# An attention and expert block on one core: a rebuilt head, half of the first attention group in step 0, and one exponential over four score banks in place of two

## The chip, the cores and the metric

The kernel runs on one core of one Trainium2 chip. Its engines work at the same time from queues of their own: TensorE (PE, with its weight loads PEld), VectorE (DVE), ScalarE (ACT), GpSimd (POOL), and SyncE (SP), which here only issues DMAs. They wait for each other on semaphores. The metric is device time in microseconds (us); lower is better. The profile is of one execution; its span runs from the first to the last instruction.

## The reference

For 16 batches of 256 tokens with 128 channels, one block of an adaptive-norm transformer in fp32:

```python
mod = (silu(c) @ wmod).reshape(16, 6, 1, 128)          # shifts, scales and gates
h = layernorm(x) * (1 + ca) + sa
q, k, v = split(h @ Wqkv + bqkv)                       # 16 heads of 8
Kmat = exp(-(|k|^2 + |q|^2 - 2 k.q) * r_sigma)         # 256 x 256 for each head, no softmax
x = x + ga * ((Kmat @ v) @ Wproj + bproj)
h = layernorm(x) * (1 + cb) + sb
mask = top2(softmax(h @ Wr.T + br))                    # 2 of 8 experts
x = x + gb * sum_e mask_e * (h @ We_e.T + be_e)
```

The gates ga and gb are pushed away from zero to at least 0.25 in size.

## The kernel before

One batch is one unit of work. The 16 heads of a batch are handled in four groups of four; a group's scores are 256 x 256 for four heads and fill four banks of PSUM (`scores`, 128 partitions x 4 banks x 512). Per group, TensorE computes the scores (`qk_scores`, line 962: eight matmuls, two token halves by four heads, each with 32 rows of `st`), ScalarE takes the exponential from PSUM into `probs` (`exp`, line 495, two instructions of 128 x 1024, one for two banks each), and TensorE multiplies with the values (`pv`, line 982, eight matmuls, four for each token half). The squares |q|^2 and |k|^2 are brought into the scores by extra rows of `st`: `st` has, for a head, the query or key in a high and a low fp32r part, and rows with the norms and with ones. These rows are gathered by DMAs (`stack` in the sync block, lines 310 to 322).

The order is written out by hand, in steps: step k does the attention of batch k, and beside it the query and key rows of batch k+1 (`qk_rows`, line 1001, and then bias, high and low parts, squares and norms), the layernorm of batch k+2, the projection and second norm of batch k-1, and router and experts of batches k-2 and k-3. Each engine has its own list for a step, with semaphore waits where it needs the others. Steps 0 to 2 lack the later parts and have less TensorE work. Ahead of step 0 is the head (steps -2 and -1): modulation, layernorm of batch 0, queries and keys of batch 0, their norms, and the DMAs that fill `st` for batch 0. At its end stands the last step (`last`) and a `tail`.

In the head, a few things matter here:

- `warm_up` (line 914) issues matmuls of the identity matrix whose results nobody reads. They stand in the head, and in step 0 three behind `qk_scores(0, 1)` and two behind `norms(1)`.
- Queries and keys of batch 0 go into one bank `qkv_ps`; VectorE adds the bias for both (`qkf`, line 714), squares both (639), and makes the low parts (641); ScalarE makes the high parts (475); TensorE makes the norms from the squares into `qkv_ps` (1023); VectorE copies their high part (726) and makes the low one (731). Then the norm rows go to `st` by a DMA from SP (317) and one from ScalarE's queue (488).
- The bias columns for queries and keys (`bias_columns`, lines 646 to 659) need `bq_all` from memory and stand behind the modulation columns (`modulation`, lines 626 and 627), which `h1` of batch 0 (553) waits for.
- VectorE clears `vpad` of batch 0 (903).
- `qk_scores` of a group waits in two places: for the exponential of the group before over banks 0 and 1 (`exp_a`) ahead of its first matmul, and over banks 2 and 3 (`exp_b`) ahead of its third:

## Time and profile before

| | us |
|---|---|
| runs | 222.79, 222.18, 224.8 |
| median | 222.79 |
| profiled execution, its device time | 223.4 |
| profiled execution, its span | 221.6 |
| PE busy in the span | 211.3 (95%) |
| DVE busy | 176.4 (80%) |
| ACT busy | 163.5 (74%) |
| POOL busy | 138.3 (62%) |

The device time of the profiled execution is 1.8 us more than its span, and 0.6 us more than the median. On the chain of work that ended last, PE has 88% of the span, ACT 3%, DVE, POOL and plain issue 2% each, DMA 1%. A matmul's shown duration is longer than the distance to the next one, since matmuls are pipelined: for how fast TensorE goes, the distance of starts counts. The view of the granted clock is in tenths of full speed; half of it is the lower of the two levels, 1.2 GHz, and all of it 2.4 GHz.

### The profile page before, as it was taken

Reading aid. Unit: us, or ns where it says so; the run is one execution under the profiler, and the core shown is the slowest. Engines: PE = TensorE matmul, PEld = TensorE weight load, DVE = VectorE, ACT = ScalarE, POOL = GpSimd, SP = SyncE. Lnnn points to the kernel's source line nnn. Section 1 sums busy time; section 2 is a strip of 40 time slices with the busy share of each in tenths; the row PEclk is TensorE's granted clock in tenths of the full one; section 3 lists DMA queues with packets and bytes.
Section 4 is the critical chain, followed back from the end, with each engine's and each line's share of the span. In section 5 each row is a group of like instructions: output and inputs, shape, how many; then the busy total and the mean of one; then the engine's idle time right before and its main releaser. Section 6 shows DMA issues by size and latency. Waiting matters only on the chain.

```text
span 221.6 us, 8225 instructions
## 1 busy us (share of the span) xinstructions
PE 211.3 (95%) x3250; PEld 148.2 (67%) x3250; DVE 176.4 (80%) x610; ACT 163.5 (74%) x234; POOL 138.3 (62%) x204
## 2 busy tenths in 40 slices
PE   7979889899999999999999999999999999999993
PEld 6656454567676767677677767676767767666791
DVE  5876442768888898988898888889898889877884
ACT  5236888877877868698877788686879777787362
POOL 5455756564957758575849486675857594434183
PEclk9996999999999999999999999999999999999999
DMA  5565233332323332434333332324341423200001
GB/s 152 150 209 180 71 114 104 114 105 104 114 74 127 106 119 86 151 89 148 96 144 74 104 129 81 125 81 143 86 151 68 149 67 120 79 24 27 3 24 49
DMA packets 22472, 22.94 MB, mean 104 GB/s; under 512 B 2330, under 2 KB 20258, under 8 KB 22434
## 3 DMA queue, kind: packets, MB, share of 16 engines
q1 hardware_dynamic: 21962, 21.79, 30.3%
q10 hardware_dynamic: 472, 0.62, 0.9%
q8 instruction: 26, 0.43, 0.8%
q14 instruction: 12, 0.10, 0.2%
HBM read 6.65 MB, written 2.12 MB: 40 GB/s over the span
## 4 chain that ended last, share of the span: by engine, by line
PE 88%; ACT 3%; issue 2%; DVE 2%; POOL 2%; DMA 1%; POOLq 0%; DVEq 0%; ACTq 0%
PE att_ps L982 26%; PE scores L962 12%; PE qkv_ps L1001 7%; PE qkv_ps L1010 4%; PE qkv_ps L1120 3%; PE mid_ps L1048 3%; PE ffn_ps L1120 3%; PE ffn_ps L1122 3%; PE ffn_ps L1121 3%; ACT probs L495 3%; PE att_ps L1120 2%; PE scores L914 2%; PE mid_ps L1084 2%; PE qkv_ps L1122 2%; PE qkv_ps L1121 2%
## 5 line engine op out<-in xcount | busy, mean ns | idle before, releaser
L495 ACT ACTIVATE probs<-scores 128x1024 f32<-128x1024 f32 x128 | 124.3, 1022 | 12.1 <-PE scores L962 7.1
L982 PE MATMUL att_ps<-probs,vpad 128*32 128x256 f32 x1024 | 68.0, 382 | 0.0
L982 PEld LDWEIGHTS att_ps<-probs,vpad 128*32 128x32 f32 x1024 | 29.6, 109 | 17.7 <-issue 0.2
L962 PE MATMUL scores<-st 32*128 32x256 f32 x512 | 37.3, 329 | 4.2 <-ACT probs L495 2.7
L368 POOL TENSOR_TENSOR ve<-stats,eps 128x2 f32<-128x2 f32 x32 | 6.3, 195 | 44.8 <-DVE stats L688 44.8
L708 DVE SCALAR_TENSOR_TENSOR acc<-ffn_ps,mask,acc 128x128 f32<-128x128 f32 x114 | 32.0, 343 | 0.2
L962 PEld LDWEIGHTS scores<-st 32*128 32x128 f32 x512 | 23.1, 183 | 13.2 <-ACT probs L495 4.7
L411 POOL TENSOR_TENSOR sq<-qkf 128x512 f32<-128x512 f32 x15 | 15.6, 1042 | 20.8 <-DVE qkf L714 20.8
L375 POOL TENSOR_SCALAR xn<-x_all,stats,rstd 128x128 f32<-128x128 f32 x30 | 25.8, 863 | 1.6
L370 POOL TENSOR_TENSOR rstd<-ve,expo 128x2 f32<-128x2 f32 x32 | 22.8, 711 | 2.5
L708 DVE SCALAR_TENSOR_TENSOR acc<-qkv_ps,mask,acc 128x128 f32<-128x128 f32 x64 | 18.0, 344 | 7.3 <-PE qkv_ps L1122 7.3
L714 DVE TENSOR_TENSOR qkf<-qkv_ps,bqk_col 128x512 f32<-128x512 f32 x16 | 11.1, 692 | 12.1 <-PE qkv_ps L1001 12.0
L413 POOL TENSOR_TENSOR hl<-qkf,hl 128x512 fp32r<-128x512 f32 x15 | 19.4, 1292 | 0.0
L1001 PE MATMUL qkv_ps<-h,wqk_sb 128*32 128x256 f32 x256 | 17.1, 385 | 0.0
L1120 PE MATMUL ffn_ps<-we_hi,h_hi 128*128 128x256 f32 x56 | 17.1, 305 | 0.0
L502 ACT COPY acc<-mid_ps 128x256 f32<-128x256 f32 x15 | 5.6, 372 | 14.8 <-PE mid_ps L1084 14.8
L1121 PE MATMUL ffn_ps<-we_hi,h_lo 128*128 128x256 f32 x56 | 15.6, 279 | 0.0
L1122 PE MATMUL ffn_ps<-we_lo,h_hi 128*128 128x256 f32 x56 | 15.6, 279 | 0.0
L708 DVE SCALAR_TENSOR_TENSOR acc<-att_ps,mask,acc 128x128 f32<-128x128 f32 x52 | 14.6, 343 | 0.2 <-DVE acc L708 0.2
L382 POOL TENSOR_TENSOR gated<-acc,rb_all 128x256 f32<-128x256 f32 x14 | 10.3, 737 | 5.2 <-DVE acc L708 4.5
L688 DVE BATCH_NORM_STATS2 stats<-x_all 128x6 f32<-128x256 f32 x32 | 12.5, 423 | 0.1
L396 POOL TENSOR_TENSOR x_all<-x_all,rb_all 128x256 f32<-128x256 f32 x16 | 11.8, 739 | 0.0
(172 smaller groups left out, 429.6 us busy)
## 6 DMA issues: line engine op xcount, KB each, us to landing
st<-hl SPq DMA_DIRECT2D x47, 256.0 KB
rb_all<-rb_rows SPq DMA_DIRECT2D x16, 192.0 KB, 3.2
out_dram<-x_all SPq DMA_DIRECT2D x16, 128.0 KB, 1.8
x_all<-in_L_attn_x_dram SPq DMA_DIRECT2D x13, 128.0 KB, 3.0
st<-norm_parts SPq DMA_DIRECT2D x60, 16.0 KB
we_sb<-in_L_ffn_w_experts_dram SPq DMA_DIRECT2D x1, 512.0 KB, 5.4
w_mod_sb<-in_L_wmod_dram SPq DMA_DIRECT2D x1, 256.0 KB, 4.6
st<-hl ACTq DMA_DIRECT2D x1, 256.0 KB
```

The costliest lines, as they stand in the source:

```text
L370: nc.gpsimd.tensor_tensor(rstd[:, n, :], ve[:, n, :], expo[:, :], ALU.pow).then_inc(rstd_ok, 1)
L375: i = nc.gpsimd.tensor_scalar(xn[:, par, t * C:(t + 1) * C], x_all[:, b, t * C:(t + 1) * C], stats[:, 0, par, 3 * t + 1:3 * t + 2], rstd[: ...
L411: nc.gpsimd.tensor_tensor(sq[:, :, :], qkf[:, :, :], qkf[:, :, :], ALU.mult).then_inc(sq_ok, 1)
L413: nc.gpsimd.tensor_tensor(hl[:, 1:4:2, :], qkf[:, :, :], hl_f[:, 0:4:2, :], ALU.subtract).then_inc(lo_ok, 1)
L495: nc.scalar.activation(probs[:, g, 2 * half:2 * half + 2, :], scores[:, 2 * half:2 * half + 2, :], ACT.Exp, scale=two_sigma).then_inc((exp ...
L708: v.scalar_tensor_tensor(acc[:, q, t, :], y, m, acc[:, q, t, :], ALU.mult, ALU.add).then_inc(acc_step, 1)
L962: i = pe.matmul(scores[:, r, t * T:(t + 1) * T], st[rows, par, g, t * P:(t + 1) * P], st[rows, par, g, T:2 * T], start=True, stop=True)
L982: i = pe.matmul(att_ps[r * ROWS:(r + 1) * ROWS, 0:T], heads[:, g * ROWS:(g + 1) * ROWS], probs[:, g, r, t * T:(t + 1) * T], start=(g == 0 ...
L1001: i = pe.matmul(qkv_ps[m, a * T:(a + 1) * T], wqk_sb[:, a, m], h1[:, :], start=True, stop=True)
L1120: pe.matmul(dst, hi, we_hi[:, es], start=True, stop=False)
L1121: pe.matmul(dst, lo, we_hi[:, es], start=False, stop=False)
L1122: i = pe.matmul(dst, hi, we_lo[:, es], start=False, stop=True)
```

## The change

Three things are changed.

1. The exponential is one instruction of 128 x 2048 over all four banks of a group. It waits for both halves of the scores (`qk_a`, `qk_b`) and signals once (`exp_done`). `qk_scores` waits once, for all of it, and its wait ahead of the third matmul is gone.
2. In step 0 the five warm-up matmuls are gone, and the first token half of `pv(0, 0)` stands where three of them stood. The other half stays where `pv(0, 0)` was.
3. The head is rebuilt. Warm-ups now use a block of zeros (`blank`), which VectorE clears as its first instruction, and do not wait for the identity matrix; they are fewer and wider, and the two behind `values(0)` are gone. Keys of batch 0 go to `att_ps` instead of `qkv_ps`, and the norms to `scores`. VectorE treats the queries and ScalarE the keys: squares, high parts and bias on each. VectorE makes both low parts, and ScalarE copies the high part of the norms. The products for the bias columns (`bias_picks`) stand ahead of `modulation(0)`; the columns made from the identity alone (`norm_columns`) stand at VectorE's start, and the copy `ident_r` behind the expert weights. Clearing `vpad` of batch 0 is split between VectorE and ScalarE. ScalarE loads its scale register ahead of the keys' parts instead of behind the DMAs, and issues its low-row DMA behind the norms' high part.

```diff
@@ scalar
+            def first_keys():
+                act.wait_ge(qk_ps, 1)
+                act.wait_ge(bqk_ok, 1)
+                nc.scalar.activation(sq[:, 1, :], k_bank(0), ACT.Square, bias=bqk_col[:, 1:2]).then_inc(sq_ok, 1)
+                nc.scalar.activation(hl[:, 2, :], k_bank(0), ACT.Identity, bias=bqk_col[:, 1:2]).then_inc(hi_ok, 1)
...
-                act.wait_ge((qk_a, qk_b)[half], n + 1)
+                act.wait_ge(qk_a, n + 1)
+                act.wait_ge(qk_b, n + 1)
                 if k > 0:
                     act.wait_ge(pv_done, n - G + 1)
-                nc.scalar.activation(probs[:, g, 2 * half:2 * half + 2, :], scores[:, 2 * half:2 * half + 2, :], ACT.Exp,
-                                     scale=two_sigma).then_inc((exp_a, exp_b)[half], 1)
+                nc.scalar.activation(probs[:, g, :, :], scores[:, :, :], ACT.Exp, scale=two_sigma).then_inc(exp_done, 1)
...
@@ scalar, last()
-                exp(b, 2, 0)
+                exp(b, 2)
                 start_acc(b - 2)
-                exp(b, 2, 1)
@@ vector
             def first_parts():
 
+                dve.wait_ge(q0_ps, 1)
+                dve.wait_ge(bqk_ok, 1)
+                v.tensor_scalar(qkf[:, 0, :], qkv_ps[:, 0:T], bqk_col[:, 0:1], None, ALU.add).then_inc(qkf_ok, 1)
                 dve.wait_ge(qkf_ok, 1)
-                v.tensor_tensor(sq[:, :, :], qkf[:, :, :], qkf[:, :, :], ALU.mult).then_inc(sq_ok, 1)
+                v.scalar_tensor_tensor(sq[:, 0, :], qkv_ps[:, 0:T], bqk_col[:, 0:1], qkf[:, 0, :], ALU.add, ALU.mult).then_inc(sq0_ok, 1)
...
                     first_normalise()
+                    bias_picks()
                     modulation(0)
...
@@ tensor
-            def warm_up(n, w=P, bank=None):
+            def warm_up(n, w=P):
 
                 for _ in range(n):
-                    pe.matmul(scores[:, R - 1, 0:w] if bank is None else bank[:, 0:w], ident[:, :], ident[:, 0:w], start=True, stop=True)
+                    pe.matmul(scores[:, R - 1, 0:w], blank[:, 0:P], blank[:, 0:w], start=True, stop=True)
...
                 if n > 0:
-                    pe.wait_ge(exp_a, n)
+                    pe.wait_ge(exp_done, n)
...
-                        if t == 0 and r == 2 and n > 0:
-                            pe.wait_ge(exp_b, n)
...
                 qk_scores(k, 1)
                 if k == 0:
 
-                    pe.wait_ge(wr_sb_ok, 1)
-                    warm_up(3, P, att_ps)
+                    pv(k, 0, (0,))
...
-                if k == 0:
-                    warm_up(2, P, att_ps)
                 qk_scores(k, 2)
-                pv(k, 0)
+                pv(k, 0, range(NT) if k > 0 else (1,))
```

VectorE's list in the head, from the two layernorm instructions of batch 0 to the norms' low part. Before:

```order
L632 TENSOR_SCALAR xn<-x_all,stats,rstd 128x128 x2
L626 COPY shift_col<-mid_ps 128x16
L627 TENSOR_SCALAR scale_col<-mid_ps 128x16
L688 BN_STATS stats<-x_all 128x6
L646 TENSOR_TENSOR bq_pick<-ident,bq_all 128x128 x2
L650 TENSOR_REDUCE nw_pick<-ident 128x16
L652 TENSOR_REDUCE bqk_col<-bq_pick 128x2
L655 TENSOR_SCALAR nw<-nw_pick 128x4x4 x2
L657 TENSOR_REDUCE lo_col<-ident 128x1
L658 TENSOR_REDUCE be_col<-ident 128x1
L659 CAST ident_r<-ident 128x128
L714 TENSOR_TENSOR qkf<-qkv_ps,bqk_col 128x512
```

Of the change, the same place:

```order
L652 TENSOR_SCALAR xn<-x_all,stats,rstd 128x128 x2
L672 TENSOR_TENSOR bq_pick<-ident,bq_all 128x128 x2
L646 COPY shift_col<-mid_ps 128x16
L647 TENSOR_SCALAR scale_col<-mid_ps 128x16
L719 BN_STATS stats<-x_all 128x6
L679 TENSOR_REDUCE bqk_col<-bq_pick 128x2
L689 TENSOR_SCALAR nw<-nw_pick 128x4x4 x2
L847 MEMSET vpad 128x640
L660 TENSOR_SCALAR qkf<-qkv_ps,bqk_col 128x256
L662 SCALAR_TENSOR_TENSOR sq<-qkv_ps,bqk_col,qkf 128x256
L663 TENSOR_SCALAR hl<-qkv_ps,bqk_col 128x256
L665 SCALAR_TENSOR_TENSOR hl<-qkv_ps,bqk_col,hl 128x256
```

`bq_pick`, which needs a loaded tensor, now stands ahead of the modulation columns; four instructions on the identity have left the place, half of the clearing of `vpad` has come in, and the work on `qkf` is by halves.

TensorE's list in step 0, from the scores of group 0 to those of group 3. Before:

```order
L962 MATMUL scores<-st 128x256 x8
L1001 MATMUL qkv_ps<-h,wqk_sb 32x256 x8
L962 MATMUL scores<-st 128x256 x8
L914 MATMUL att_ps<-ident 128x128 x3
L1023 MATMUL qkv_ps<-sq,nw 32x128 x4
L914 MATMUL att_ps<-ident 128x128 x2
L962 MATMUL scores<-st 128x256 x8
L982 MATMUL att_ps<-probs,vpad 32x256 x8
L1010 MATMUL qkv_ps<-wqkv_sb,h 32x128 x8
L982 MATMUL att_ps<-probs,vpad 32x256 x8
```

Of the change:

```order
L991 MATMUL scores<-st 128x256 x8
L1030 MATMUL qkv_ps<-h,wqk_sb 32x256 x8
L991 MATMUL scores<-st 128x256 x8
L1010 MATMUL att_ps<-probs,vpad 32x256 x4
L1055 MATMUL qkv_ps<-sq,nw 32x128 x4
L991 MATMUL scores<-st 128x256 x8
L1010 MATMUL att_ps<-probs,vpad 32x256 x4
L1041 MATMUL qkv_ps<-wqkv_sb,h 32x128 x8
L1010 MATMUL att_ps<-probs,vpad 32x256 x8
```

The five warm-ups are gone and four matmuls of `pv(0, 0)` have moved up past the norms and the scores of group 2.

## Rows read from the trace of the kernel before

**Rows 1.** The page: PE's granted clock in 40 slices, tenths of full speed.
```profile
PEclk9996999999999999999999999999999999999999
```

**Rows 2.** Busy time by stretch: length, PE, PEld, DVE, ACT, POOL, clock, DMA, GB/s.
```profile
14.65:27.00 12.35, 10.99 (x140) 6.74 (x144) 6.25 (x10) 8.78 (x11) 7.22 (x8) 0.86 0.36 117
27.00:36.60 9.60, 8.35 (x148) 4.61 (x140) 3.69 (x9) 7.83 (x10) 6.09 (x10) 1.00 0.29 96
109.00:121.00 12.00, 12.00 (x204) 8.41 (x204) 10.57 (x37) 9.61 (x14) 8.31 (x13) 1.00 0.37 112
```

**Rows 3.** Timeline, a full step: start, length, engine, line, instruction.
```profile
109.43 1.94 ACT L495 ACTIVATE probs<-scores 128x1024 f32<-128x1024 f32 x2
111.72 0.51 PE L962 MATMUL scores<-st 32*128 32x256 f32 x8
```

**Rows 4.** Timeline of the head.
```profile
1.51 1.97 PE L914 MATMUL scores<-ident 128*128 128x128 f32 x8 [1.51 <-POOL ident L352]
1.95 1.12 DVE L903 MEMSET vpad<- 128x1280 f32 x1 [0.22 <-issue]
2.10 0.43 SPq L292 DMA_DIRECT2D bq_all<-in_L_attn_bqkv_dram  x1
...
5.98 0.17 DVE L626 COPY shift_col<-mid_ps 128x16 f32<-128x16 f32 x1 [0.85 <-PE mid_ps L926]
6.49 0.56 ACT L553 ACTIVATE h<-qkv_ps,shift_col,scale_col 128x256 f32<-128x256 f32 x1 [1.01 <-PE qkv_ps L1035]
6.49 0.65 DVE L646 TENSOR_TENSOR bq_pick<-ident,bq_all 128x128 f32<-128x128 f32 x2
7.23 1.07 PE L1001 MATMUL qkv_ps<-h,wqk_sb 128*32 128x256 f32 x16
8.37 0.69 DVE L714 TENSOR_TENSOR qkf<-qkv_ps,bqk_col 128x512 f32<-128x512 f32 x1
8.67 0.71 PE L914 MATMUL scores<-ident 128*128 128x128 f32 x4
9.84 0.63 PE L1023 MATMUL qkv_ps<-sq,nw 128*32 128x256 f32 x4 [0.46 <-DVE sq L639]
10.52 0.42 DVE L726 CAST norm_hi<-qkv_ps 64x256 fp32r<-64x256 f32 x1
10.97 0.47 DVE L731 SCALAR_TENSOR_TENSOR norm_parts<-norm_hi,lo_col,qkv_ps 64x256 fp32r<-64x256 f32 x1
11.47 1.18 ACTq L488 DMA_DIRECT2D st<-norm_parts  x1
14.66 0.51 PE L962 MATMUL scores<-st 32*128 32x256 f32 x8 [1.21 <-DMA st<-norm_parts]
```

**Rows 5.** DMA issues of the head: KB, us from issue to landing.
```profile
bq_all<-in_L_attn_bqkv_dram SPq DMA_DIRECT2D x1, 192.0 KB, 3.9
```

**Rows 6.** Timeline of step 0.
```profile
15.20 1.94 ACT L495 ACTIVATE probs<-scores 128x1024 f32<-128x1024 f32 x2 [0.85 <-PE scores L962]
17.63 1.94 ACT L495 ACTIVATE probs<-scores 128x1024 f32<-128x1024 f32 x2 [0.49 <-PE scores L962]
17.71 1.65 PE L914 MATMUL att_ps<-ident 128*128 128x128 f32 x6
20.98 0.51 PE L962 MATMUL scores<-st 32*128 32x256 f32 x8
22.78 0.59 SPq L321 DMA_DIRECT2D st<-norm_parts  x1
26.70 1.94 ACT L495 ACTIVATE probs<-scores 128x1024 f32<-128x1024 f32 x2
```

**Rows 7.** Busy time of one stretch in step 0, columns as in rows 2.
```profile
18.00:19.00 1.00, 1.00 (x6) 1.00 (x5) 1.00 (x2) 1.00 (x2) 1.00 (x2) 0.50 0.46 150
```

**Rows 8.** Timeline, one exponential of two banks alone.
```profile
15.20 1.02 ACT L495 ACTIVATE probs<-scores 128x1024 f32<-128x1024 f32 x1 [0.85 <-PE scores L962]
```

**Rows 9.** Timeline of the last step.
```profile
200.55 0.37 ACT L502 COPY acc<-mid_ps 128x256 f32<-128x256 f32 x1 [0.43 <-PE mid_ps L1084]
```

More of the change, by code:

```diff
@@ L186, in adaln_block @@
         h1_ok = sem("h1_ok")
+        blank_ok = sem("blank_ok")
+        q0_ps = sem("q0_ps")
+        sq0_ok = sem("sq0_ok")
+        hi0_ok = sem("hi0_ok")
+        lo0_ok = sem("lo0_ok")
+        vpad0_ok = sem("vpad0_ok")
         qk_ps = sem("qk_ps")
@@ L200, in adaln_block @@
         qk_b = sem("qk_b")
-        exp_a = sem("exp_a")
-        exp_b = sem("exp_b")
+        exp_done = sem("exp_done")
         pv_done = sem("pv_done")
@@ L267, in b_bank, with k_bank, n_bank @@
             return mid_ps[:, 0:NT * C] if b < NB - 1 else scores[:, 2, 0:NT * C]
+        def k_bank(b):
+            return att_ps[:, 0:T] if b == 0 else qkv_ps[:, T:2 * T]
+        def n_bank(b):
+            return scores[:, 0, :] if b == 0 else qkv_ps
         def norm_tile(b):
@@ L723, in norm_rows @@
             def norm_rows(b):
-                dve.wait_ge(n_ps, b + 1)
-                if b == 0:
-                    v.tensor_copy(norm_hi[norm_tile(b)], qkv_ps[norm_tile(b)]).then_inc(nh_ok, 1)
                 dve.wait_ge(nh_ok, b + 1)
@@ L730, in norm_rows @@
                 tile = norm_tile(b)
-                v.scalar_tensor_tensor(norm_parts[tile], norm_hi[tile].bitcast(F32), lo_col[tile[0], :], qkv_ps[tile],
+                v.scalar_tensor_tensor(norm_parts[tile], norm_hi[tile].bitcast(F32), lo_col[tile[0], :], n_bank(b)[tile],
                                        ALU.mult, ALU.add).then_inc(norm_ok, 1)
@@ L735, in values @@
                 dve.wait_ge(v_ps, b + 1)
-                if b == 1:
-                    dve.wait_ge(vpad1_ok, 1)
+                if b < 2:
+                    dve.wait_ge((vpad_ok, vpad1_ok)[b], 1)
+                if b == 0:
+                    dve.wait_ge(vpad0_ok, 1)
                 v.tensor_tensor(vpad[:, b % 2, :, :, 0:HD],
@@ L968, in pv @@
                 if 0 in halves:
-                    pe.wait_ge(exp_a, G * b + g + 1)
-                    pe.wait_ge(exp_b, G * b + g + 1)
+                    pe.wait_ge(exp_done, G * b + g + 1)
                     if g == 0:
@@ L999, in qk_rows @@
                 for a in range(2):
+                    dst = (qkv_ps[:, 0:T], k_bank(b))[a]
                     for m in strips():
-                        i = pe.matmul(qkv_ps[m, a * T:(a + 1) * T], wqk_sb[:, a, m], h1[:, :], start=True, stop=True)
+                        i = pe.matmul(dst[m, :], wqk_sb[:, a, m], h1[:, :], start=True, stop=True)
+                    if b == 0 and a == 0:
+                        i.then_inc(q0_ps, 1)
                 i.then_inc(qk_ps, 1)
@@ L1022, in norms @@
                     a, t = j % 2, j // 2
-                    i = pe.matmul(qkv_ps[j * ROWS:(j + 1) * ROWS, tokens], nw[:, :, :, :].rearrange("p r i g -> p (r i g)"),
+                    i = pe.matmul(n_bank(b)[j * ROWS:(j + 1) * ROWS, tokens], nw[:, :, :, :].rearrange("p r i g -> p (r i g)"),
                                   sq[:, a, t * n:(t + 1) * n], start=True, stop=True)
```

88 lines of the change are left out of this document (46 added, 42 removed).

## The prediction

> **What bounds the kernel now.** I read the busy time by stretch first. In a full step TensorE is busy for all 12.00 of 12.00 us, ScalarE for 9.61 [rows 2]; there the time is the number of TensorE's instructions and nothing else. It is different in step 0 (10.99 of 12.35, and part of this is warm-up) and step 1 (8.35 of 9.60) [rows 2], and in the head, up to 14.66, where the first scores start behind a DMA [rows 4]. Next I read the timeline of a full step for slack: the pair of exponentials of group 0 starts at 109.43 and ends at 111.37; the scores of the next group start at 111.72 [rows 3]. So TensorE comes 0.35 us later than ScalarE would let it, and by the timeline this is the smallest such gap of a full step. Then the timelines of the head and of step 0, where latencies rule. The granted clock is full nearly everywhere, except one slice in step 0 [rows 1], where a whole microsecond reads 0.50 [rows 7], that is 1.2 GHz.
>
> So the change can win or lose in the head, in steps 0 to 2 and in the last step. About thirteen full steps of 12 us should stay as they are.
>
> **The exponential in one piece.** 128 x 1024 takes 1.02 us [rows 8], the pair 1.94 [rows 6], so the second adds 0.92. 128 x 2048 is not in the trace. Its bounds are 1.84 (twice the increment) and 1.94 (no gain over the pair); I take 1.88, since some fixed part must remain. Where ScalarE sets the pace, groups start 17.63 - 15.20 = 2.43 apart [rows 6]: 1.94 for the pair, 0.05 for the signal, 0.44 from the scores' third matmul to the next exponential. After the change TensorE starts all eight matmuls at the end, and the exponential waits for the last, which costs 0.54 (14.66 to 15.20 [rows 4, 6]). The period becomes 1.88 + 0.05 + 0.54 = 2.47, 0.04 longer (0.00 to 0.10 by the bounds). TensorE itself loses nothing: the six matmuls behind `exp_b` hold it as long as all eight would, since four with different rows run together. Outside step 0 I count two or three such groups, in steps 1 and 2 and the last: **+0.1**. In full steps 0.35 of slack covers it, and nothing changes. If the cover were gone, each 0.1 us over it would cost 0.4 us a step.
>
> In the last step the copy `acc` (line 502) stood at 200.55, between the two halves of an exponential [rows 9]; it took 0.37 and ended at 200.92. Now it stands behind the whole exponential, which I work out to end at about 201.0, so it ends at 201.4. The transposition `turn_x2`, which waits for it, is due at about 201.2 on a TensorE that is full from there on: **+0.2** (0 to +0.4).
>
> **The head.** `bq_all` is issued at 2.10 and needs 3.9 us [rows 4, 5], so it lands at 6.0. VectorE now waits for it ahead of the modulation columns, which before ran at 5.98 [rows 4]. The two products take 0.65, the two columns 0.25: ready at 6.9, and `h` starts at 6.9 instead of 6.49. It takes 0.56, and the query rows start at 7.5 instead of 7.23 (before, warm-ups held them until then) [rows 4]: 0.3 late. This is taken back behind it. Behind the columns VectorE drops four instructions of 0.2 to 0.4 each and takes on half of a clearing of 1.12 [rows 4], so it is free at about 8.1; the query half is there at 8.1 too, half of 1.07 later plus the signal. Then bias 0.42, squares 0.42 (sizes of 128 x 256; the nearest row is 0.42 for `norm_hi`), norms 0.63, `norm_hi` 0.42, `norm_parts` 0.47 [rows 4], with 0.05 between: 8.15 + 2.36 + 0.2 = 10.7. VectorE's three other parts (1.2 us) run under norms and `norm_hi`; ScalarE's square and high part of the keys, 8.6 to 9.7 even at the 0.56 of `h`, come in time. Before, `norm_parts` ended at 10.97 + 0.47 = 11.44. So the norm rows' DMA, issued at 11.47 before [rows 4], goes 0.7 earlier. But the larger DMAs of high and low rows ahead of it are only about 0.3 earlier (high parts are done at 9.5 to 9.7 instead of 9.7), and what follows takes from 11.47 to 14.6 with the DMA engines full for most of it. I take **-0.4** for the first scores. The bounds: -0.75 if the last issue sets it, and +0.4 if nothing behind the late `h` is taken back.
>
> **Step 0.** Before, the scores of group 2 start at 20.98 [rows 6]. The exponential of group 1 ended at 19.57; ten more warm-up instructions (five matmuls in two passes each) and the norms stood ahead on TensorE, at half clock for the most part. Without them the scores start at 19.6, 1.35 earlier. Counted from the first scores (14.66), the exponentials then start at 0.54, 3.0, 5.5 and 8.0. Between scores 2 and scores 3 stand half of `pv(0, 0)`, values and `pv(0, 1)`, by their distances in full steps 0.45, 0.5 and 0.9: done at 7.3, just under the exponential. The next step's scores could start at 9.95. What is late next is `st` of batch 1: its last norm DMA was issued at 22.78 [rows 6], 8.12 after the first scores; it stands in SP's queue behind the low rows, which wait for POOL, and POOL is not moved. I give it 0.2. With 2.5 us to land that is 10.4, and the exponential of step 1 starts at 10.95 against 12.04 before (26.70 [rows 6]). -1.1, and 0.1 back for half clock on the scores: **-1.0**. The bounds: -0.5 if landing takes 3.1 as in the head (11.47 to 14.6 [rows 4]), -1.6 if the DMAs are in time. Step 1 and what follows move as a block.
>
> **The sum.** -0.4 - 1.0 + 0.1 + 0.2 = -1.1. Against the profiled execution, 223.4 (span 221.6 and 1.8 around it), that gives 222.3; that execution was 0.6 above the median of 222.79, so for the median I forecast **221.7**. Differences of under about 2% (4.5 us) can hardly be told from no change here.
>
> **Rivals.** *The clock, slower.* The warm-ups are there to keep TensorE at 2.4 GHz, and even with them it read 0.50 in step 0 [rows 7]. The head's first four warm-up matmuls took 1.97 us, four later ones 0.71 [rows 4]: TensorE began slow and got fast in the head. With `h` later and fewer warm-ups it may be slow when it comes to query rows and norms. These hold TensorE for about 0.9 and 0.4 us at full clock, so +1.3, and in step 0 the work between scores 2 and 3 (1.85) comes out from under the exponential by 1.0 or more. 222.8 - 1.1 + 1.3 + 1.0 = 224.0. It decides once slow time on the path beyond that of before exceeds 2.2 us, since half of it is lost. Against it: `pv` and scores are real work that moves up into the same place. Chance 0.14.
> The Trainium skill (TensorE: Matmul & The Clock Gate, "What's actually happening") says that the throttled state is the default and activity releases it. The two warm-up rows agree with it, and by that rule this rival is a question of how much work is left in the head.
>
> *The gain is given back at the DMAs.* `st` of batch 1 lands as late as before, and the head gains nothing because its DMAs are full: -0.5 + 0.3 = -0.2, 222.6. The DMA wait of 1.21 ahead of the first scores [rows 4] speaks for it. Chance 0.2.
>
> *More than that.* Head at -0.75, step 0 at -1.6, last step at 0: -2.3, 220.5. Chance 0.15.
>
> *ScalarE becomes the bound of full steps.* It would need an exponential of 1.94 + 0.35 = 2.29 us; twice 1.02 is 2.04, even with no overlap at all. At 2.35 it would be 13 x 4 x 0.06 = +3, 225. Chance 0.02.
>
> **How the numbers follow.** My forecast has 0.48, from 221.0 to 222.3, the rivals 0.14, 0.2, 0.15 and 0.02; 0.01 is left. The range of 8 in 10 reaches from the third rival's 220.3 to most of the clock's, 223.7. No case reaches 2% by itself; for what I have not seen I leave 0.05 for faster and 0.04 for slower, and 0.91 for within 2%.
>
> **What would show it.** In the changed profile: modulation columns at about 6.7 and `h` at 6.9 (bias products first); `norm_parts` done by 10.8; first scores at 14.1 to 14.4; an exponential of 128 x 2048 at 1.88; exponentials of step 0 about 2.5 apart; the first of step 1 about 11 us after the first scores, behind a DMA wait; a full step of 12.06 us still, with TensorE full; ScalarE's `acc` copy in the last step behind the exponential. I am wrong if full steps change at all, if the granted clock reads 0.5 in the head, or if step 0 keeps its length.

## The result and the profile after

The changed kernel takes 225.44 us (median of 14 runs), the kernel before beside it 223.0 (14 runs). The ratio is 1.008, with an interval of 1.006 to 1.011: slower by a little under 1%, where I had forecast 0.5% faster. The profiled execution of the changed kernel took 224.6, with a span of 222.4 (before: 223.4 and 221.6). Of the difference of 1.2 us, 0.8 lie in the span and 0.4 outside it. (The ratios here leave out executions more than 1.5% above the fastest of their kernel; means are over all.)

Timeline of the head of the changed kernel (start, length, engine, line, instruction, idle time before and what ended it), beside [rows 4]:

```profile
1.44 2.07 PE L944 MATMUL scores<-blank 128*128 128x512 f32 x2 [1.44 <-DVE blank L930]
...
5.60 0.68 DVE L672 TENSOR_TENSOR bq_pick<-ident,bq_all 128x128 f32<-128x128 f32 x2 [0.44 <-DMA bq_all<-in_L_attn_bqkv_dram]
6.19 0.17 DVE L646 COPY shift_col<-mid_ps 128x16 f32<-128x16 f32 x1
6.54 0.56 ACT L576 ACTIVATE h<-qkv_ps,shift_col,scale_col 128x256 f32<-128x256 f32 x1 [0.41 <-PE qkv_ps L1066]
7.26 1.08 PE L1030 MATMUL qkv_ps<-h,wqk_sb 128*32 128x256 f32 x8
8.11 1.08 PE L1030 MATMUL att_ps<-h,wqk_sb 128*32 128x256 f32 x8
8.41 0.48 DVE L660 TENSOR_SCALAR qkf<-qkv_ps,bqk_col 128x256 f32<-128x256 f32 x1 [0.49 <-PE qkv_ps L1030]
...
9.82 0.60 PE L1055 MATMUL scores<-sq,nw 128*32 128x256 f32 x4
10.87 0.47 DVE L757 SCALAR_TENSOR_TENSOR norm_parts<-norm_hi,lo_col,scores 64x256 fp32r<-64x256 f32 x1 [0.15 <-ACT norm_hi L503]
11.38 1.17 ACTq L513 DMA_DIRECT2D st<-norm_parts  x1
14.74 0.51 PE L991 MATMUL scores<-st 32*128 32x256 f32 x8 [1.34 <-DMA st<-norm_parts]
```

The waited-for product `bq_pick` stands ahead of the modulation columns, and here `bq_all` came early (5.60). Even so, `norm_parts` is done at 11.34, only 0.1 earlier than before, and the first scores are 0.08 later. The query and key rows run at half speed: two blocks of 1.08 where sixteen matmuls took 1.07 before.

The page's row of PE's granted clock (40 slices, in tenths; beside [rows 1]), and the same as busy time by stretch: step 0, step 1, a full step, and the slow part of step 0 (length, PE, PEld, DVE, ACT, POOL, clock, DMA, GB/s; beside [rows 2, 7]):

```profile
PEclk9995899999999999999999999999999999999999
```

```profile
14.74:27.33 12.59, 9.64 (x126) 5.17 (x130) 6.21 (x10) 8.12 (x6) 7.22 (x8) 0.73 0.37 125
27.00:36.60 9.60, 8.02 (x155) 4.48 (x147) 3.67 (x9) 7.39 (x7) 5.70 (x9) 1.00 0.27 93
109.00:121.00 12.00, 12.00 (x202) 8.44 (x202) 10.57 (x38) 9.45 (x10) 8.32 (x12) 1.00 0.34 114
16.70:23.40 6.70, 5.43 (x64) 3.18 (x68) 3.96 (x8) 4.48 (x4) 4.38 (x6) 0.50 0.43 153
```

The full step is unchanged: TensorE has 12.00 of 12.00. In step 0 TensorE is busy for 1.35 us less than in [rows 2], and yet the step is no shorter: the clock is at 0.50 (1.2 GHz) for 6.8 us of it; before, it was for 3.4. The prediction had named "step 0 keeps its length" as a sign that it is wrong, and here it is.

The exponentials of step 0, the first of step 1, and the last step (beside [rows 6, 9]):

```profile
15.39 1.88 ACT L522 ACTIVATE probs<-scores 128x2048 f32<-128x2048 f32 x1 [2.05 <-PE scores L991]
18.27 1.88 ACT L522 ACTIVATE probs<-scores 128x2048 f32<-128x2048 f32 x1 [1.00 <-PE scores L991]
21.15 1.88 ACT L522 ACTIVATE probs<-scores 128x2048 f32<-128x2048 f32 x1 [0.84 <-PE scores L991]
24.67 1.88 ACT L522 ACTIVATE probs<-scores 128x2048 f32<-128x2048 f32 x1 [1.65 <-PE scores L991]
27.33 1.88 ACT L522 ACTIVATE probs<-scores 128x2048 f32<-128x2048 f32 x1 [0.33 <-PE scores L991]
...
201.56 0.37 ACT L528 COPY acc<-mid_ps 128x256 f32<-128x256 f32 x1
202.07 0.41 PE L1087 MATMUL mid_ps<-ident,x2n 128*128 128x128 f32 x2 [0.16 <-ACT acc L528]
204.06 1.88 ACT L522 ACTIVATE probs<-scores 128x2048 f32<-128x2048 f32 x1 [0.97 <-PE scores L991]
```

The first exponential is 0.19 later than before, that of step 1 0.63 later (27.33 against 26.70), the last of all 0.96 later (204.06 against 203.10).

### The profile page after: what moved, and what is told of

Read it like the earlier page. It is cut to its first block, busy times and chain, and to the rows that moved or that the text cites. A ratio compares the mean times of both kernels' runs of the same rounds, so it can differ in the third digit from the quotient of the medians.

```text
span 222.4 us, 7994 instructions
## 1 busy us (share of the span) xinstructions
PE 209.2 (94%) x3224; PEld 143.5 (64%) x3224; DVE 176.0 (79%) x612; ACT 161.2 (72%) x173; POOL 138.1 (62%) x204
## 4 chain that ended last, share of the span: by engine, by line
PE 88%; ACT 7%; issue 2%; DMA 1%; DVE 1%; SPq 1%; ACTq 0%
PE att_ps L1010 26%; PE scores L991 13%; PE qkv_ps L1030 7%; ACT probs L522 6%; PE qkv_ps L1041 4%; PE mid_ps L1079 3%; PE ffn_ps L1151 3%; PE qkv_ps L1151 3%; PE ffn_ps L1152 3%; PE ffn_ps L1153 3%; PE att_ps L1151 2%; PE scores L944 2%; PE qkv_ps L1153 2%; PE mid_ps L1115 2%; PE qkv_ps L1152 2%
## 5 line engine op out<-in xcount | busy, mean ns | idle before, releaser
L522 ACT ACTIVATE probs<-scores 128x2048 f32<-128x2048 f32 x64 | 120.3, 1880 | 20.0 <-PE scores L991 19.6
L1010 PE MATMUL att_ps<-probs,vpad 128*32 128x256 f32 x1024 | 69.4, 388 | 0.0
L991 PE MATMUL scores<-st 32*128 32x256 f32 x512 | 35.8, 332 | 7.5 <-ACT probs L522 6.2
L991 PEld LDWEIGHTS scores<-st 32*128 32x128 f32 x512 | 22.5, 187 | 15.9 <-ACT probs L522 7.3
L743 DVE TENSOR_TENSOR qkf<-qkv_ps,bqk_col 128x512 f32<-128x512 f32 x15 | 10.4, 691 | 12.8 <-PE qkv_ps L1030 12.8
L784 DVE TENSOR_SCALAR x2n<-x_all,stats,rstd 128x128 f32<-128x128 f32 x32 | 9.6, 343 | 2.7 <-POOL rstd L385 1.4
```

The lines of the kernel that those rows point to most:

```text
L522: nc.scalar.activation(probs[:, g, :, :], scores[:, :, :], ACT.Exp, scale=two_sigma).then_inc(exp_done, 1)
L991: i = pe.matmul(scores[:, r, t * T:(t + 1) * T], st[rows, par, g, t * P:(t + 1) * P], st[rows, par, g, T:2 * T], start=True, stop=True)
L1010: i = pe.matmul(att_ps[r * ROWS:(r + 1) * ROWS, 0:T], heads[:, g * ROWS:(g + 1) * ROWS], probs[:, g, r, t * T:(t + 1) * T], start=(g == 0 ...
```

## The experiments

All on one core. "Low" counts the executions whose mean granted clock over the span was under 0.995; every profile of such an execution has a stretch at 1.2 GHz in the first steps, or (f1) in the head. "Span, not low" is the mean span of the others. "Outside" is device time less span. Each difference is to the runs of before of its own call.

| kernel | runs | mean us | to before | ratio, interval | outside | low | span, not low |
|---|---|---|---|---|---|---|---|
| before | 159 | 223.1 | | | 1.81 | 60 of 159 | 220.7 |
| after | 14 | 225.3 | +2.1 | 1.008, 1.006 to 1.011 | 2.22 | 12 of 14 | 223.3 |
| e1 one exponential | 12 | 223.8 | +0.6 | 1.002, 0.998 to 1.006 | 1.81 | 5 of 12 | 221.1 |
| e2 step 0 | 12 | 223.5 | +0.2 | 1.001, 0.998 to 1.004 | 1.83 | 10 of 12 | 220.8 |
| e3 head | 12 | 224.7 | +1.5 | 1.005, 1.001 to 1.009 | 2.19 | 7 of 12 | 222.0 |
| e4 head, step 0 | 12 | 224.1 | +0.8 | 1.005, 1.001 to 1.008 | 2.20 | 8 of 12 | 222.3 |
| f1 after, one wait | 12 | 224.2 | +1.0 | 1.004, 0.999 to 1.008 | 2.22 | 6 of 12 | 221.7 |
| f2 after, fill | 12 | 225.3 | +2.0 | 1.005, 1.000 to 1.010 | 2.19 | 8 of 12 | 222.4 |
| f3 step 0, fill | 12 | 223.3 | 0.0 | 1.001, 0.998 to 1.005 | 1.82 | 9 of 12 | 220.1 |
| f4 unused semaphores | 8 | 223.0 | -0.2 | 0.999, 0.995 to 1.003 | 1.81 | 2 of 8 | 220.8 |
| g1 warm-ups alone | 12 | 223.1 | +0.2 | 1.000, 0.998 to 1.002 | 1.84 | 7 of 12 | 220.5 |
| g2 new head, old warm-ups | 8 | 223.7 | +0.8 | 1.006, 1.004 to 1.009 | 2.16 | 1 of 8 | 221.5 |
| g3 old head, one wait | 12 | 223.2 | +0.3 | 1.001, 0.998 to 1.005 | 1.80 | 8 of 12 | 220.5 |
| g4 before, fill | 12 | 223.3 | +0.4 | 1.002, 0.999 to 1.005 | 1.81 | 6 of 12 | 220.7 |
| h1 after, picks back | 12 | 224.2 | +1.2 | 1.006, 1.002 to 1.009 | 2.21 | 11 of 12 | 220.6 |
| h2 head, step 0, picks back | 12 | 224.0 | +0.9 | 1.002, 0.997 to 1.006 | 2.19 | 10 of 12 | 219.6 |
| h3 before, square | 10 | 223.0 | 0.0 | 0.999, 0.994 to 1.003 | 1.83 | 4 of 10 | 220.8 |
| h4 after, no square | 10 | 224.6 | +1.6 | 1.007, 1.003 to 1.011 | 2.18 | 7 of 10 | 223.2 |
| i1 head, picks back, old warm-ups | 12 | 222.6 | -0.3 | 1.000, 0.997 to 1.003 | 2.19 | 1 of 12 | 220.3 |
| i2 as i1, with step 0 | 12 | 223.3 | +0.3 | 1.001, 0.998 to 1.004 | 2.01 | 10 of 12 | 220.0 |

A mean over 12 runs is uncertain by 0.2 to 0.4 (standard error), so single differences under about 0.7 decide nothing.

### One part at a time

**e1**, the exponential alone, with its semaphores; of its edit, the waits:

```diff
-                act.wait_ge((qk_a, qk_b)[half], n + 1)
+                act.wait_ge(qk_a, n + 1)
+                act.wait_ge(qk_b, n + 1)
...
```

> The kernel before with only the exponential made one instruction over four banks (both waits, one signal, the copy of acc behind it). Theory A (the exponential is the loss): its start is 0.15 us behind the last score matmul instead of 0.04, as in the changed kernel, so a group paced by ScalarE is 2.58 apart instead of 2.43, and the last step loses 0.3 to 0.5 at the copy; together 0.6 to 1.2 us slower than before, ratio 1.003 to 1.005. Theory B (the clock in step 0 is the loss): this run is within 0.3 us of before. Theory C (the head is the loss): the same, within 0.3 us.

**e2**, step 0 alone:

```diff
-                    pe.wait_ge(wr_sb_ok, 1)
-                    warm_up(3, P, att_ps)
+                    pv(k, 0, (0,))
...
-                    warm_up(2, P, att_ps)
...
-                pv(k, 0)
+                pv(k, 0, range(NT) if k > 0 else (1,))
```

> The kernel before with only step 0 changed: five warm-up matmuls out, the first token half of pv(0, 0) in their place. Theory B: the granted clock stays at half for a longer stretch than before (two thirds of step 0 instead of a quarter), and the run is 0.5 to 1.5 us slower than before. Theory A or C: TensorE comes to the scores of group 2 about 1.3 us earlier, and the run is 0.5 to 1.3 us faster than before.

**e3**, the whole head alone (the change without the two edits above), and **e4**, head and step 0 together. Of the head, the places that matter below:

```diff
                     first_normalise()
+                    bias_picks()
                     modulation(0)
...
                 values(0)
-                warm_up(2)
                 norms(0)
```

> The kernel before with only the head rebuilt; step 0 and the exponentials are those of before (warm-ups on the block of zeros). Theory C: first scores no earlier, and the run slower than before by 0.5 us or more, for instance because TensorE is at half clock longer in the head or in step 0. Theory A or B: first scores within 0.1 us of those of before, and the time within 0.3 us of it.

> The changed kernel with the exponential in two again (two signals, two waits in the scores, the copy of acc between the halves). Theory A: at or under the time of before, 1 us or more faster than the changed kernel. Theory B or C: still 1 us or more slower than before.

Measured: +0.6, +0.2, +1.5 and, together, +0.8. The three parts add up to 2.3, and the change cost 2.1. The head is the largest. It also brings all of the 0.4 outside the span: 2.2 in e3 and e4, 1.8 in e1 and e2. Timeline of e3's head:

```profile
7.07 0.66 DVE L680 TENSOR_TENSOR bq_pick<-ident,bq_all 128x128 f32<-128x128 f32 x2 [1.91 <-DMA bq_all<-in_L_attn_bqkv_dram]
7.65 0.16 DVE L654 COPY shift_col<-mid_ps 128x16 f32<-128x16 f32 x1
7.99 0.56 ACT L580 ACTIVATE h<-qkv_ps,shift_col,scale_col 128x256 f32<-128x256 f32 x1 [1.86 <-DVE scale_col L655]
8.61 1.08 PE L1041 MATMUL qkv_ps<-h,wqk_sb 128*32 128x256 f32 x8 [1.28 <-ACT h L580]
16.32 0.51 PE L1001 MATMUL scores<-st 32*128 32x256 f32 x8 [1.39 <-DMA st<-norm_parts]
```

Here the products on `bq_all` start at 7.07, after VectorE has stood still for 1.91, and `h` starts at 7.99. The first scores are at 16.32. e4 shows the same (7.00, 16.40).

### The waits, the fill, unused semaphores

**f1**, the changed kernel with the exponential's first wait left out (the second implies it, since TensorE signals `qk_a` first):

```diff
-                act.wait_ge(qk_a, n + 1)
                 act.wait_ge(qk_b, n + 1)
```

> The changed kernel; the exponential waits only for the signal of the last score matmul (qk_b), no longer for qk_a as well. Theory A (the second wait is dear): the exponential starts 0.04 to 0.05 us behind the last score matmul instead of 0.15, and the span shrinks by 0.1 for each group that ScalarE paces, 0.6 to 0.9 us in all. If the second wait is not the cause of the late start: no change, the exponential still 0.15 behind.

**f2**, the changed kernel, and **f3**, the kernel before with the change's step 0, each with four warm-ups at the end of the head:

```diff
                 turn_x(1)
                 expert_weights()
+                warm_up(4)
```

> The changed kernel with four more warm-up matmuls behind the expert weights' transpositions, where TensorE waits about 1.3 us for the DMA of the norm rows; they hold it for about 0.9 us. Theory B (clock): TensorE keeps the full clock through step 0 in most executions, most mean clocks at 0.997 or more, and the mean span falls by 1 us or more. Rival: the clock was hidden under the exponentials anyway; less than 0.3 us.

> The kernel before with step 0 as in the change (no warm-ups, first half of pv(0, 0) moved up) and four warm-up matmuls in TensorE's wait for the first norm rows. Theory B: without the low clock in step 0 the 1.0 us that the prediction gave to step 0 shows: mean time 0.8 to 1.5 us under that of before, and no executions about 2 us above the rest. Rival (the move of pv itself gains nothing, because DMAs bind): within 0.4 us of the fast executions of before.

**f4**, the kernel before with five semaphores that nothing uses:

```diff
+        unused = [sem(f"unused{i}") for i in range(5)]
```

> The kernel before with five more semaphores that nobody uses, as many as the change has more in all. In all executions with the rebuilt head the device time is 2.2 us above the span, in all others 1.8. Theory D (it is the number of semaphores): 2.1 to 2.3 here. Rival (it is something else of the head, such as what starts first or the code): 1.8 here.

f1 gained 1.1 against the changed kernel. Its exponentials in step 0 (timeline):

```profile
16.52 1.88 ACT L521 ACTIVATE probs<-scores 128x2048 f32<-128x2048 f32 x1 [1.55 <-PE scores L990]
19.03 1.88 ACT L521 ACTIVATE probs<-scores 128x2048 f32<-128x2048 f32 x1 [0.64 <-PE scores L990]
21.55 1.88 ACT L521 ACTIVATE probs<-scores 128x2048 f32<-128x2048 f32 x1 [0.48 <-PE scores L990]
```

2.52 apart at full clock. With both waits and full clock (f2) they start at 17.05, 19.64 and 22.22, 2.58 to 2.59 apart. So the second wait costs 0.06 to 0.07 in a group that ScalarE paces. In these two profiles it makes 0.33 from the first scores to the first exponential of step 1 (10.74 against 11.07), 0.11 in steps 1 to 3 and 0.06 in the last step, 0.5 together; the rest of the 1.1 is within what two means can differ by, and f1 also had fewer low executions. f2 gained nothing, although its profile shows full clock in step 0: its `h` was late (`bq_pick` at 6.96), and the first scores came at 16.39. f3's profile has its low stretch in step 1 (26.1 to 29.5): the fill did not take it away. It need not have moved it either, since the profiles of f4 and g1, without any fill, have theirs in step 1 too. f4 changed nothing outside the span, nor its mean beyond the error, and so gave a second profile of the kernel before, with full clock in step 0. Its timeline:

```profile
15.44 0.51 PE L963 MATMUL scores<-st 32*128 32x256 f32 x8 [1.13 <-DMA st<-norm_parts]
18.42 1.94 ACT L496 ACTIVATE probs<-scores 128x1024 f32<-128x1024 f32 x2 [0.50 <-PE scores L963]
19.63 0.71 PE L915 MATMUL att_ps<-ident 128*128 128x128 f32 x4
20.27 0.64 PE L963 MATMUL scores<-st 32*128 32x256 f32 x8
20.86 1.94 ACT L496 ACTIVATE probs<-scores 128x1024 f32<-128x1024 f32 x2 [0.34 <-PE scores L963]
26.41 1.93 ACT L496 ACTIVATE probs<-scores 128x1024 f32<-128x1024 f32 x2
```

The warm-ups run here in time: the scores of group 2 start at 20.27, before the exponential of group 1 ends at 20.36, and the exponentials are 2.44 apart with all warm-ups in place. From the first scores to the first exponential of step 1 it is 10.97, not the 12.04 of [rows 6]. The same stretch in e2, with the change's step 0:

```profile
14.88 0.51 PE L962 MATMUL scores<-st 32*128 32x256 f32 x8 [1.10 <-DMA st<-norm_parts]
25.50 1.93 ACT L495 ACTIVATE probs<-scores 128x1024 f32<-128x1024 f32 x2
```

10.62. At full clock the change's step 0 gains 0.35. Six profiles with the old step 0 at full clock and two exponentials have 10.92 to 10.97 (f4, g1, g2, g4, h3, i1), and three with the new one 10.61 or 10.62 (e2, e4, f3). But e2's profile gives it back one step later, at the DMAs of batch 2, which the prediction had feared for batch 1:

```profile
36.78 0.51 PE L962 MATMUL scores<-st 32*128 32x256 f32 x8 [1.23 <-DMA st<-norm_parts]
```

From the first exponential of step 1 to that of step 4 e2 takes 35.58, 1.1 more than the profile of the kernel before (34.47), with the clock full. i2 has the same wait (1.24). The kernel before has none there, nor have e4 and the changed kernel; e1, g2, g3 and h3 have 0.17 to 0.50.

### Warm-ups or the late h

**g1**, the kernel before with the change's blank block and its fewer, wider warm-ups:

```diff
-                warm_up(3)
-                warm_up(1, P // 2)
+                pe.wait_ge(blank_ok, 1)
+                warm_up(1, 4 * P)
...
-                warm_up(2)
                 norms(0)
```

**g2**, the reverse: the new head with all old warm-ups.

```diff
-                warm_up(1, 3 * P)
+                warm_up(3)
...
                 values(0)
+                warm_up(2)
                 norms(0)
```

> The kernel before with one part of the head's rebuilding alone: the block of zeros and the fewer, wider warm-ups (the two behind values(0) gone); everything else in the head as before. The head alone gave a device time 0.4 us longer outside the span, a full clock only from 11.5 us on, and a mean 1.5 us worse. Theory A (fewer warm-up instructions in the head delay the full clock): full clock at 11 us or later here, first scores at 15.8 or later, mean 0.7 to 1.2 above the kernel before. Theory B (the late h and the order of VectorE's work delay it): full clock by 9.5, first scores by 15.5, mean within 0.3 of before. The 0.4 outside the span: theory C (it comes with the new first instructions and buffer) 2.2 outside here; theory D (it comes with something else of the head) 1.8.

> The kernel before with the rebuilt head but the old warm-ups (identity, the old number and sizes, the two behind values(0) back; the block of zeros is still cleared first, since vpad is cleared from it); exponential and step 0 as before. Theory A (warm-ups): full clock by 9.5, first scores at 15.5 or earlier, mean within 0.5 of before. Theory B (late h, order): full clock at 11 or later, first scores 15.9 or later, mean about 1.5 above before as with the whole head. Theory C for the time outside the span: 1.8 to 2.2, by whether the buffer or the warm-ups make it; theory D: 2.2.

**g3**, old head, the change's step 0 and the one exponential with one wait; **g4**, the kernel before with f2's fill.

> The old head with the change's step 0 and the one exponential, which waits for the second half of the scores only. If the head is what costs, and the second wait most of the rest, this should be as fast as the kernel before: mean within 0.4, exponentials of step 0 2.5 apart, 1.8 outside the span. If the one exponential itself costs (last step, scores behind the whole of it), 0.5 to 0.9 above before.

> The kernel before with four more warm-ups (128 columns, eight instructions) behind the last work of the head, in the wait of 1.2 us for the first scores' rows. If the half clock in steps 0 and 1 comes from TensorE's idling there, the mean falls by 0.5 or more, since the spans of 222 to 223 go away and those of 220 to 221.4 stay. If TensorE falls to half clock wherever it has gaps, in steps 0 and 1 too, the spans keep two groups and the mean is within 0.3 of before. Half clock on the warm-ups would make the first scores up to 0.4 later.

g1 fell on theory B's side: +0.2, first scores at 14.06. That early start is not its edit's merit: g4, whose head has all the old warm-ups, had 14.14. g2 lies between the two theories: +0.8, of which 0.35 is outside the span, with matmuls at full speed only from about 10 us on and only 1 low execution of 8. Neither theory stands as it was put, but the 0.4 outside the span came with g2 and not with g1, so theory C is out. g3 is within its error of the kernel before: with the change's step 0 beside it, one exponential with one wait costs little or nothing. g4 brought no gain, and kept low executions.

Within the new head the first scores sort by one thing. In seven profiles the products stand ahead of the columns (after, e3, e4, f1, f2, g2, h4). In two of these `bq_all` let them start at 5.6, and the first scores came at 14.7; in five they started at 6.6 to 7.1, and the first scores came at 15.65 to 16.40. In the four with the products behind the columns (h1, h2, i1, i2, below) they came at 14.61 to 14.85. With the old order `bq_all` was as late in e1 and f3 (7.0), and the modulation columns ran at 5.98 all the same.

The old head varies too, by something else: over its nine profiles the first scores lie from 14.06 to 15.52. In the four at 15.23 or later (f3, f4, g3, h3) the query and key matmuls took 1.94, at half speed; in the four at 14.73 or earlier they took 1.07; e2 stands between (1.40, 14.88). In the new head they ran at half speed in after, g2, h2 and i2, and the first scores still came at 14.70 to 14.85. So a single profile of the head tells little.

### Taking the wait out

**h1**, the changed kernel, and **h2**, e4's kernel, with this edit:

```diff
-                    bias_picks()
                     modulation(0)
+                    bias_picks()
```

**h3**, the kernel before with one square of a number on ScalarE, and **h4**, the changed kernel without its square:

```diff
-                nc.scalar.activation(sq[:, 1, :], k_bank(0), ACT.Square, bias=bqk_col[:, 1:2]).then_inc(sq_ok, 1)
+                nc.scalar.activation(sq[:, 1, :], k_bank(0), ACT.Identity, bias=bqk_col[:, 1:2]).then_inc(sq_ok, 1)
```

> The changed kernel with the two products on bq_all put back behind the modulation columns of batch 0; everything else stays. Theory A (the wait for bq_all ahead of the modulation columns is what the head costs inside the span): modulation columns at about 5.6, h by 6.5 whether bq_all lands at 5.6 or at 7.0, first scores by 15.0, and the mean 0.7 to 1.0 below the changed kernel's 225.3, at 224.3 to 224.6. Theory B (the clock in the head, or the order behind h, costs it): mean within 0.3 of the changed kernel's. Outside the span 2.2 by both.

> Rebuilt head and step 0 of the change, the exponential in two pieces as before, and the products on bq_all behind the modulation columns. Without the move this kernel had a mean of 224.05, 0.8 above before. Theory A: 0.7 to 1.0 less, 223.1 to 223.4, the span's mean 0.2 to 0.6 under the kernel before's, and the rest of the difference is the 0.4 outside the span. Theory B: 223.8 or more.

> The kernel before with one more instruction on ScalarE in the head: the square of one number, 1 x 1, whose result nobody reads. If the 0.4 us outside the span hang on that function (another program part or table that is made ready before the first instruction), device time less span is 2.2 here; if not, 1.8. Inside the span nothing changes by either.

> The changed kernel with the plain bias addition in place of the square of the keys of batch 0 on ScalarE, so that the norms of the keys of batch 0 are made from the keys and not from their squares; times of all instructions should be as in the changed kernel. If the 0.4 us outside the span hang on the square function, device time less span is 1.8 here and the mean about 0.4 below the changed kernel's 225.3; if not, 2.2 and the same mean within 0.3.

Timeline of h1:

```profile
6.01 0.17 DVE L646 COPY shift_col<-mid_ps 128x16 f32<-128x16 f32 x1 [0.85 <-PE mid_ps L956]
6.52 0.56 ACT L576 ACTIVATE h<-qkv_ps,shift_col,scale_col 128x256 f32<-128x256 f32 x1 [0.38 <-PE qkv_ps L1066]
6.61 0.67 DVE L672 TENSOR_TENSOR bq_pick<-ident,bq_all 128x128 f32<-128x128 f32 x2 [0.35 <-DMA bq_all<-in_L_attn_bqkv_dram]
14.64 0.51 PE L991 MATMUL scores<-st 32*128 32x256 f32 x8 [1.38 <-DMA st<-norm_parts]
```

`bq_all` was late again (6.61), and now `h` does not wait for it. h1's mean is 1.1 below that of the changed kernel, in the place and size that theory A gave; among low executions alone the mean spans are 222.2 and 223.1. h2's mean is the same as e4's within the error (224.0 and 224.1), which is theory B's side of its expectation: the head's part is there (first scores at 14.85, not 16.40), but 10 of its 12 executions were low, and they were no shorter than e4's 8 (222.2 against 221.6). Its two others had spans of 219.4 and 219.8, 1.1 under the 220.7 of the kernel before. So the mechanism holds in both pairs, the gain in time in one. The next section has a third pair. The square is not what the outside time hangs on: 1.83 with it, 2.18 without.

### The clock's share, and the best version

**i1**, new head, products behind the columns, all old warm-ups, old step 0, two exponentials (g2's kernel with h1's edit). **i2**, the same with the change's step 0, and with `vpad` cleared by VectorE alone:

```diff
+            v.memset(vpad[:, 0, :, :, :].rearrange("p t h w -> p (t h w)"), 0.0).then_inc(vpad_ok, 1)
...
-            clear()
```

> Rebuilt head with the products on bq_all behind the modulation columns and with all old warm-ups; step 0 and exponential as before. If the late h and the loss of warm-ups are all that the head costs inside the span, the span's mean is 0.2 to 0.7 under that of the kernel before (h at 6.5, norm_parts done by 11.5), with half-clock stretches in no more executions than before (about 4 in 10). Device time: 0.4 outside is still there, so 222.8 to 223.3 against 223.1. If the order behind h costs something too, the span's mean is equal or above.

> As the kernel of the run before it, with the change's step 0 (no warm-ups there, half of pv(0, 0) moved up), and with vpad of batch 0 cleared by VectorE alone at its old place, so that the block of zeros and ScalarE's clearing are gone. If step 0's real work keeps TensorE at full clock, the span's mean falls by a further 0.4, and half-clock stretches stay at 4 in 10; if the lost warm-ups of step 0 are what makes them more frequent, 6 to 9 in 10 executions show one and the mean does not fall. Device time less span: 1.8 if the extra time outside the span hangs on ScalarE's clearing, 2.2 if not.

Against g2, from which it differs only by the place of the products, i1's mean is 1.1 lower (222.6 and 223.7). Both had one low execution, and in the others the mean spans are 220.3 and 221.5. This is the cleanest measure of the wait, since the clock has no part in it.

i1 is the fastest kernel of the study by its mean: 222.6, 0.3 under the kernel before in spite of the 0.4 outside the span. Its span is 0.7 shorter: 0.4 by the head (220.3 against 220.7 where the clock stayed full), the rest because only 1 execution of 12 was low. By the interval of its ratio it cannot be told from the kernel before. Its page's clock row, and its head:

```profile
PEclk9999999999999999999999999999999999999999
```

```profile
10.71 0.47 DVE L765 SCALAR_TENSOR_TENSOR norm_parts<-norm_hi,lo_col,scores 64x256 fp32r<-64x256 f32 x1
14.61 0.51 PE L1001 MATMUL scores<-st 32*128 32x256 f32 x8 [1.38 <-DMA st<-norm_parts]
```

i2 shows what step 0 does beyond its own length: a further 0.3 off the span where the clock stayed full (220.0), and 10 of 12 executions low, so the mean is worse by 0.6. The 0.3 rests on the two executions that were not low. Over all kernels, low executions are 93 of 245 (38%) where step 0 has its warm-ups, and 99 of 132 (75%) where it has not. In the kernel before, a low execution has a span 1.6 longer. In the changed kernel it is not longer: its 12 low executions have a mean span of 223.1, its two others 223.3.

The profiles by stretch, from differences of start times ("exponential" is the first of its step; "low" says where the granted clock read 0.50):

| profile | low | first scores | to exponential of step 1 | from there to that of step 4 |
|---|---|---|---|---|
| before | step 0 | 14.66 | 12.04 | 34.47 |
| h3 (as before) | none | 15.52 | 10.96 | 34.69 |
| f4 (as before) | step 1 | 15.44 | 10.97 | 36.26 |
| i1 | none | 14.61 | 10.92 | 34.57 |
| e2 new step 0 | none | 14.88 | 10.62 | 35.58 |
| e4 new step 0 | none | 16.40 | 10.61 | 34.58 |
| after | step 0 | 14.74 | 12.59 | 34.61 |
| f2 as after | none | 16.39 | 11.07 | 34.73 |
| f1 one wait | head | 15.93 | 10.74 | 34.62 |
| i2 | step 0 | 14.73 | 11.79 | 35.42 |

A low stretch cost 1.1 in step 0 of the kernel before (12.04 against 10.97), 1.5 in that of the changed kernel (12.59 against 11.07), and 1.6 in step 1 (36.26 against 34.69).

## Why the prediction was wrong

The forecast was -1.1; the change costs +2.1 on the mean. Step by step:

- **bq_all lands at 6.0: this step failed, and the largest single part of the loss is here.** I took one transfer's landing in one execution as its time. Over all 20 profiles it took 3.2 (e2) to 5.0 (f1) from issue to landing, where [rows 5] has 3.9, and the products that wait for it start anywhere from 5.6 to 7.1. When it is late, all of it passes on: `h` at 7.5 to 8.0 instead of 6.9, first scores 1.4 later on average (16.1 against 14.7). The bound I gave (+0.4, "if nothing behind the late `h` is taken back") was too small, since it knew only the landing of [rows 5]. Five late of seven, by 1.4, is +1.0; moving the products back took 1.1 off in h1 and 1.1 in i1, and nothing in h2.
- **The rest of the head: right in size once the wait is gone.** i1's head gains 0.4 at full clock, as forecast. VectorE's pieces took 0.48 each, where I had 0.42, and the query and key rows ran at half clock in the profile of the changed kernel; with the loss of both, `norm_parts` came only 0.1 earlier. Norm rows' issue to first scores took 3.36 (before 3.19), so the DMAs gave some of it back, as the second rival had it. i1 and g2 show it more strongly: `norm_parts` was done at 11.18 and 12.18, and the first scores came at 14.61 and 14.70.
- **Outside the span: +0.4, not in the forecast at all.** It sits in every kernel with the new head, and neither the square, the block of zeros with its warm-ups, nor unused semaphores make it. Its cause is open. It is 1.80 to 1.84 with 110 to 112 semaphores in use, 2.01 with 115, and 2.16 to 2.22 with 116 and 117. It rises with the number in use, but not evenly (0.2 from 115 to 116, nothing from 116 to 117), no run varied that number alone, and i2 also lacks ScalarE's clearing. The Trainium skill (Runtime: NRT & Kernel Launch, The ~15µs preamble/postamble breakdown) lists a reset of the user semaphores before and after a kernel; no run here shows that reset itself.
- **Step 0, -1.0: the term was mis-sized; it is -0.35.** I priced the five warm-ups by [rows 6, 7], which were at half clock. At full clock they fit under the exponential (f4), and the gap I meant to close is not there. Together with the slower pace of the one exponential (next but one), the changed kernel's step 0 gains nothing at full clock: 11.07 in f2 against 10.97. The end of the chain that I gave, 10.95 from the first scores, is about right (10.62 in e2, 11.07 in f2), but the start, 12.04, was a slow instance of 10.97. I expected a DMA wait ahead of the first scores of step 1; none shows there, but e2 and i2 have one of 1.2 a step later, which takes more than the 0.35.
- **The clock, slower (a rival, 0.14): half of it is what happened.** Not the head's warm-ups by themselves (g1 +0.2), but step 0's: without them a stretch at 1.2 GHz comes in 75% of the executions, with them in 38%. The pairs that differ in little else agree: 10 of 12 in i2 and 1 of 12 in i1, 10 of 12 in e2 and 17 of 35 in the kernel before beside it. I argued that real work moving up takes their place; i2 and e2 show that it does not. In the changed kernel's profile the low stretch in step 0 is twice as long as before (6.8 against 3.4). The Trainium skill (TensorE: Matmul & The Clock Gate, Part 1: The HAM clock gate) warns that the moment at which matmuls get fast differs from run to run of one kernel. The trace agrees: the query and key matmuls, from 7.23 on in both, took 1.07 in [rows 4] and 1.94 in f4, whose instructions are the same.
- **One exponential: its price in step 0 was mis-sized.** 128 x 2048 took 1.88, as I chose. But I took 0.54 from the start of the scores to the exponential; with the second wait it is 0.65 (14.74 to 15.39), with one wait 0.59 (f1). The pace at full clock is 2.58, not 2.47, against 2.43 with two exponentials. In step 0 that is 0.45 (f2's 11.07 against e2's 10.62). Outside it, in steps 1 to 3, the +0.1 was right: 34.61 to 34.74 with one exponential and both waits (after, e1, f2, h1), 34.46 to 34.69 with two. e1 measured +0.6 in all, g3, which also has the new step 0, +0.3 with one wait.
- **Last step, +0.2: right.** The `acc` copy went from 200.55 to 201.56, `turn_x2` waited for it (0.16), and the last exponential lost another 0.25 beyond the 0.71 that it was late by at step 4 (49.82 against 49.11).
- **Full steps: right.** Five of them, to 109.43 and 110.16, took 60.32 before and 60.34 after, TensorE full, the slack covers the longer exponential. ScalarE did not become the bound.

The sum in hindsight: +0.4 outside, +1.0 for the late `bq_all`, -0.4 for the rest of the head, -0.35 for step 0, +0.6 for the exponential, +0.2 for the last step (part of e1's +0.6, so not added twice) is +1.25. Low executions going from 38% to 86%, at 1.6 each, would add 0.8 and make 2.0, of 2.1 measured. But this last term is not shown: in the changed kernel low executions were no longer than the others. The -0.4 was measured in i1 with all warm-ups in place, so the rest could as well stand there. The terms are sums of uncertain means; the late `bq_all`, the 0.4 outside, step 0 at full clock and the clock's frequency in step 0 are shown by more than one pair of runs. A slip in the recorded text: its range begins at "the third rival's 220.3", and that rival was worked out to 220.5.

## What to carry over

A wait moved ahead of critical work is priced by how late its transfer can land, not by when it landed in one trace; [rows 5] is one draw, and a landing near the moment of need deserves two prices. A piece of work that looks late in a stretch at half clock must be looked at again at full clock before its removal is given a gain, and a kernel whose executions differ by the clock in one step needs two profiles. Warm-ups that seem to lie on the path may still pay, by what they do to the clock later: i1, which kept them all, was the only rebuilt version with a mean under the kernel before's, though not by more than the error. Step 0's own gain can also be lost a step later, at the next transfer.

## What was not expected of the hardware

- A second semaphore wait of ScalarE ahead of an instruction, already satisfied or nearly so, costs 0.06 to 0.07 us where ScalarE sets the pace (2.58 in f2 against 2.52 in f1, which differ by this wait and f2's fill).
- The same DMA, issued at about 2.1, takes from 3.2 to 5.0 us to land over the profiles (`bq_all`, 192 KB); the products that wait for it started at 5.60 in the changed kernel and at 7.12 in f1.
- Early in the head the spacing of matmuls tells TensorE's speed, and the granted clock does not. The sixteen query and key matmuls took 1.07 in [rows 4] and 1.94 in f4, the same code, and f4's clock reads 1.00 in that stretch (timeline, and busy time by stretch with columns as above):

```profile
7.23 1.94 PE L1002 MATMUL qkv_ps<-h,wqk_sb 128*32 128x256 f32 x16
```

```profile
7.20:9.10 1.90, 1.90 (x21) 0.96 (x24) 1.10 (x7) 0.00 (x0) 1.79 (x3) 1.00 0.68 189
```

- Time outside the span is steady for one kernel (within 0.2, in i2 within 0.3) and differs by 0.4 between kernels.
